# A second pair of PSUM banks for the gate and up matmuls of a quantized FFN, and the pending transposes emitted ahead of the quantizer

## The chip, the cores and the metric

The kernel runs on all 8 cores of one Trainium2 chip. Each core computes one half (2048 tokens) of one of four batch entries, all cores run the same program, and none waits for another. The metric is the device time in microseconds of the slowest core.

## The reference

One layer: a layer norm, multi-head attention with a low-rank key and value, and a gated FFN whose activations and weights are quantized to blocks of 16 FP4 values. The three are added. The change lies in the FFN.

```python
def fp4_quant_dequant(x):                    # blocks of 16 along the last dim
    scale = jnp.maximum(jnp.max(jnp.abs(xb), axis=-1, keepdims=True) / 6.0, 1e-12)
    idx = jnp.searchsorted(_MID, jnp.abs(xb / scale))
    return _GRID[idx] * jnp.sign(xb / scale) * scale
def fp4_linear(x, w):
    return jnp.einsum('bsk,nk->bsn', fp4_quant_dequant(x), fp4_quant_dequant(w))
gate = fp4_linear(xn, w_gate)                # 1024 -> 2816
y = fp4_linear(xn, w_up)                     # 1024 -> 2816
ffn = fp4_linear(jax.nn.silu(gate) * y, w_down)   # 2816 -> 1024
x = x + attention(xn) + ffn
```

## The kernel before

The kernel is written with one instruction queue for each engine, filled by hand in program order (`eb.em`), and with semaphores (`eb.wait`, `then_inc`). An engine runs its queue in order. Earlier stages norm and quantize the tokens, quantize the three weight matrices, do the attention, and leave the residual in HBM. The last stage, from about 2,940 us of the span on, is the FFN.

It runs over two groups `ig` of 1408 hidden columns. For each it loads the quantized weights with transposing DMAs (`wgq_b`, `wuq_b`, `wdq_b`), and then takes the tokens in two halves of 1024. A half has 8 tiles (`tt`) of 128 tokens, and behind them the down projection of the half (L1068, with the add of the residual at L1081).

A tile goes through these steps:

- Three chunks (`ci`) of 512, 512 and 384 hidden columns, here called c0, c1 and c2. For each, TensorE runs 8 gate matmuls into the bank `pg` (L1007) and 8 up matmuls into the bank `py` (L1011). ScalarE takes Silu of `pg` into `gs_c` (L1023), and VectorE multiplies it with `py` into `h_t` (L1027) and counts `hbld` up. `pg` and `py` are the banks `psD0` and `psD1` for each chunk, and chunk number `s_` (counted through the group) waits until `hbld` has the multiply of chunk `s_` - 1 (L1005). `gs_c` has one buffer, so a Silu waits for the multiply before it (L1021).
- `emit_quant` on `h_t`. ScalarE makes Abs and Sign of the whole tile (L189, L192) once c2's multiply is through (L1032). VectorE runs 13 passes over 1408 columns or over the 88 scales: L212, L217 and L222 need only `h_t`, L227 needs Sign, L233 needs Abs, and the rest (L235 to L254) follow one another, up to `hq_t`. Then `hq` counts up.
- `emit_tr`, the transposes of the tile, is put off by one tile: the call stands in `pend_tr` and is emitted one tile later. It emits 11 transposes in groups of 4, 4 and 3 (L962), which take the banks `psA` and `psB` in turn, and for each group an eviction by ScalarE to `hqT_b` (L973). A group waits for the eviction of the group two before it. `emit_tr` emits nothing for VectorE, and `emit_quant` nothing for TensorE.

So TensorE's queue holds, for tile t: c0, c1, c2, and the transposes of tile t-1. ScalarE's holds the three Silus, Abs and Sign of tile t, and the evictions of tile t-1. VectorE's holds the three multiplies and the quantizer. The first tile of a half has no pending transposes, and those of the last are emitted behind it, ahead of the down projection. The banks `psE` and `psF` belong to the attention and stand unused in this stage.

Of the kernel before, what the change touches and what calls it, by code (L numbers as in the profile page):

```python
# [82 lines left out]
def build_program(debug=False, stop_after=9):  # L83
# [46 lines left out]
    S = {}  # L130
# [43 lines left out]
    psD0 = ps_([128, 512], F32, es_ps, "psD0")  # L174
    psD1 = ps_([128, 512], F32, es_ps, "psD1")
    psE = ps_([128, 512], F32, es_ps, "psE")
    psF = ps_([128, 512], F32, es_ps, "psF")
# [131 lines left out]
    eb = EB(nc)  # L309
# [135 lines left out]
    eb = EB(nc)  # L445
# [140 lines left out]
    eb = EB(nc)  # L586
# [251 lines left out]
    eb = EB(nc)  # L838
# [136 lines left out]
    for ig in range(2):  # L975
        i0 = IG[ig]
        if True:
            if ig > 0:
                eb.wait('sync', S['ffdn'], S['ffdn'].n)
            for kc2 in range(KC):  # L980
                S['fw'].n += 16
                eb.em('sync', lambda e, kc2=kc2, i0=i0: e.dma_start(  # L982
                    out=wgq_b[:, kc2, :], in_=WgqN[i0:i0 + 1408, kc2 * 128:(kc2 + 1) * 128], transpose=True).then_inc(S['fw'].h, 16))
            for kc2 in range(KC):
                S['fw'].n += 16
                eb.em('sync', lambda e, kc2=kc2, i0=i0: e.dma_start(  # L986
                    out=wuq_b[:, kc2, :], in_=WuqN[i0:i0 + 1408, kc2 * 128:(kc2 + 1) * 128], transpose=True).then_inc(S['fw'].h, 16))
            for it in range(11):
                S['fw'].n += 16
                eb.em('sync', lambda e, it=it, i0=i0: e.dma_start(  # L990
                    out=wdq_b[:, it, :], in_=WdqN[0:1024, i0 + it * 128:i0 + (it + 1) * 128], transpose=True).then_inc(S['fw'].h, 16))
            eb.wait('tensor', S['fw'], S['fw'].n)
            eb.wait('tensor', S['xqr'], S['xqr'].n)
        hb_base = S['hbld'].n
        for half in range(2):
            toff = half * 1024
            eb.wait('scalar', S['avq'], S['avq'].n)
            for tt in range(8):
                eb.wait('vector', S['aab'], S['aab'].n)
                for ci, (c0, clen) in enumerate(NCH):  # L1000
                    s_ = half * 24 + tt * 3 + ci
                    pg = psD0
                    py = psD1
                    if s_ >= 1:
                        eb.wait('tensor', S['hbld'], hb_base + s_)  # L1005
                    for kc2 in range(KC):
                        eb.em('tensor', lambda e, tt=tt, c0=c0, clen=clen, kc2=kc2, pg=pg, toff=toff: e.matmul(  # L1007
                            pg[:, 0:clen], xqT_sb[:, kc2, toff + tt * 128:toff + (tt + 1) * 128],
                            wgq_b[:, kc2, c0:c0 + clen], start=(kc2 == 0), stop=(kc2 == KC - 1)))
                    for kc2 in range(KC):  # L1010
                        ins = (lambda e, tt=tt, c0=c0, clen=clen, kc2=kc2, py=py, toff=toff: e.matmul(  # L1011
                            py[:, 0:clen], xqT_sb[:, kc2, toff + tt * 128:toff + (tt + 1) * 128],
                            wuq_b[:, kc2, c0:c0 + clen], start=(kc2 == 0), stop=(kc2 == KC - 1)))
                        if kc2 == KC - 1:
                            S['ffh'].n += 1
                            eb.em('tensor', lambda e, ins=ins: ins(e).then_inc(S['ffh'].h, 1))
                        else:
                            eb.em('tensor', ins)
                    eb.wait('scalar', S['ffh'], S['ffh'].n)
                    if S['hbld'].n > 0:  # L1020
                        eb.wait('scalar', S['hbld'], S['hbld'].n)  # L1021
                    S['sil'].n += 1
                    eb.em('scalar', lambda e, clen=clen, pg=pg: e.activation(  # L1023
                        out=gs_c[:, 0:clen], in_=pg[:, 0:clen], func=AF.Silu).then_inc(S['sil'].h, 1))
                    eb.wait('vector', S['sil'], S['sil'].n)
                    S['hbld'].n += 1
                    eb.em('vector', lambda e, c0=c0, clen=clen, py=py: e.tensor_tensor(  # L1027
                        out=h_t[:, c0:c0 + clen], in0=gs_c[:, 0:clen], in1=py[:, 0:clen],
                        op=ALU.mult).then_inc(S['hbld'].h, 1))
                lg = lgq  # L1030
                eb.wait('scalar', S['hq'], S['hq'].n)
                eb.wait('scalar', S['hbld'], S['hbld'].n)  # L1032
                eb.wait('vector', S['hbld'], S['hbld'].n)
                if lg >= 2:
                    eb.wait('vector', S['fftr'], 3 * (lg - 1))
                last = emit_quant(eb, 1408, h_t[:, 0:1408], hq_t[:, lg % 2, 0:1408], PL5, act_abs=True)
                S['hq'].n += 1
                eb.em('vector', lambda e, last=last: last(e).then_inc(S['hq'].h, 1))
                if pend_tr is not None:
                    pend_tr()  # L1040
                pend_tr = (lambda lg=lg, tt=tt, hq_tgt=S['hq'].n: emit_tr(eb, lg, tt, hq_tgt))
                lgq += 1
            if pend_tr is not None:
                pend_tr()
                pend_tr = None
            if debug and half == 0 and ig == 0:
                eb.wait('sync', S['fftrev'], S['fftrev'].n)
                S['out'].n += 16
                eb.em('sync', lambda e: e.dma_start(out=dbg['hq0'], in_=hqT_b[:]).then_inc(S['out'].h, 16))
                eb.wait('vector', S['out'], S['out'].n)  # L1050
            dn_base = S['ffdn'].n
            st_ds = DS['rsd'] if ig == 0 else DS['ost']
            rr_base_i = DS['rr'].cnt
            st_base_i = st_ds.cnt
            for m in range(2):
                DS['rr'].issue(eb, 'sync', rbuf[:, m % 2, :], resid_scr[m * 128:(m + 1) * 128, toff:toff + 1024])
            eb.wait('tensor', S['fftrev'], S['fftrev'].n)
            eb.wait('tensor', S['hbld'], S['hbld'].n)
            DS['rsd'].wait_all(eb, 'vector')
            DS['ost'].wait_all(eb, 'vector')  # L1060
            for m in range(8):
                for n2 in range(2):
                    idx = m * 2 + n2
                    pb = [psC0, psC1][idx % 2]
                    if idx >= 2:
                        eb.wait('tensor', S['ffdn'], dn_base + idx - 1)
                    for it in range(11):
                        ins = (lambda e, m=m, n2=n2, it=it, pb=pb: e.matmul(  # L1068
                            pb[:, :], wdq_b[:, it, m * 128:(m + 1) * 128], hqT_b[:, it, n2 * 512:(n2 + 1) * 512],
                            start=(it == 0), stop=(it == 10)))  # L1070
                        if it == 10:
                            S['avq'].n += 1
                            eb.em('tensor', lambda e, ins=ins: ins(e).then_inc(S['avq'].h, 1))
                        else:
                            eb.em('tensor', ins)
                    eb.wait('vector', S['avq'], S['avq'].n)
                    DS['rr'].wait_for(eb, 'vector', rr_base_i + m)
                    if m >= 2 and n2 == 0:
                        st_ds.wait_for(eb, 'vector', st_base_i + m - 2)
                    S['ffdn'].n += 1  # L1080
                    eb.em('vector', lambda e, m=m, n2=n2, pb=pb: e.tensor_tensor(  # L1081
                        out=obuf[:, m % 2, n2 * 512:(n2 + 1) * 512], in0=rbuf[:, m % 2, n2 * 512:(n2 + 1) * 512],
                        in1=pb[:, :], op=ALU.add).then_inc(S['ffdn'].h, 1))
                eb.wait('sync', S['ffdn'], dn_base + 2 * (m + 1))
                if ig == 0:
                    st_ds.issue(eb, 'sync', resid_scr[m * 128:(m + 1) * 128, toff:toff + 1024], obuf[:, m % 2, :])
                else:
                    st_ds.issue(eb, 'sync', o_out[m * 128:(m + 1) * 128, toff:toff + 1024], obuf[:, m % 2, :])
                if m + 2 < 8:
                    DS['rr'].issue(eb, 'sync', rbuf[:, m % 2, :], resid_scr[(m + 2) * 128:(m + 3) * 128, toff:toff + 1024])  # L1090
            if ig == 0:
                DS['rsd'].wait_all(eb, 'sync')
# [48 lines left out]
```

## Time and profile before

| | us |
|---|---|
| median of the runs | 4250.61 |
| lowest and highest | 4248.65, 4252.58 |
| the profiled execution, slowest core | 4251.97 |
| its span, first to last instruction (core 5) | 4250.3 |
| spans of the 8 cores | 4235.1 to 4250.3 |
| mean granted TensorE clock, each core | 0.829 to 0.830 |

The page gives for each engine its busy time and its share of the span, and then groups of instructions by the line of the kernel, with the engine's idle time ahead of them and the instruction that ended it ("<-" and a name is the releaser). The timeline lists instructions in order of time, alike neighbours merged: start, length, engine, line, operation, output <- inputs, count, and in brackets the idle time of the engine before it. The windows view gives, for stretches of time, the busy time of each engine and the clock granted to TensorE as a share of 2.4 GHz (0.50 is 1.2 GHz).

### The profile page before, as it was taken

How to read it: one execution, taken by the hardware profiler on the slowest of the kernel's cores; microseconds unless marked ns; L12 is line 12 of the kernel's file. 1: busy time of each engine (PE TensorE's matmuls, PEld its weight loads, DVE VectorE, ACT ScalarE, POOL GpSimd, SP SyncE). 2: the span in 40 equal slices, each digit the busy share in tenths (PEclk: the TensorE clock that was granted, in tenths of full speed). 3: DMA queues.
4: the chain of work that ended last, by engine and by line, in shares of the span. 5: the costliest groups of instructions: out<-in, count | busy, mean ns of one | idle time of the engine just before them, and what ended most of it. 6: DMA issues, size and time to landing. Idle time of an engine off the chain costs nothing. (4 is left out here: it accounts for less than half of the span.)

```text
span 4250.3 us, 36150 instructions; the slowest of 8 cores (4235.1 to 4250.3 us)
## 1 busy us (share of the span) xinstructions
PE 2578.5 (61%) x9848; PEld 946.4 (22%) x9848; DVE 2505.1 (59%) x4009; ACT 1185.1 (28%) x1835; POOL 105.7 (2%) x199
## 2 busy tenths in 40 slices
PE   1112185159696978789696969686355555245646
PEld 1112131012121222222121212232122222122222
DVE  7888803757767675857476674231365554365564
ACT  1111121035454545445454545200121111111111
POOL 0000000000000000000000000000000000000000
PEclk9999996569797988979797979778677777677878
DMA  1112130001000010101010000215301002400102
GB/s 50 30 30 66 52 47 1 19 19 36 23 30 28 27 34 19 39 16 38 17 35 19 30 23 21 40 65 168 57 0 50 30 0 82 79 0 25 55 0 69
DMA packets 126529, 156.29 MB, mean 37 GB/s; under 512 B 77824, under 2 KB 88320, under 8 KB 124288
## 3 DMA queue, kind: packets, MB, share of 16 engines
q1 hardware_dynamic: 110368, 127.56, 10.8%
q0 software_dynamic: 15968, 26.42, 2.6%
q8 instruction: 89, 1.46, 0.2%
q14 instruction: 104, 0.85, 0.1%
HBM read 98.89 MB, written 46.66 MB: 34 GB/s over the span
## 5 line engine op out<-in xcount | busy, mean ns | idle before, releaser
L1007 PE MATMUL psD<-wgq_b,xqT_sb 128*128 128x512 bf16 (+1 forms) x768 | 252.4, 491 | 503.5 <-DVE h_t L1027 376.7
L765 ACT ACTIVATE pbuf<-psA,negB_col 128x512 bf16<-128x512 f32 x512 | 351.4, 686 | 349.4 <-PE psA L751 349.4
L765 ACT ACTIVATE pbuf<-psB,negB_col 128x512 bf16<-128x512 f32 x512 | 351.2, 686 | 289.0 <-PE psB L751 288.1
L1027 DVE TENSOR_TENSOR h_t<-gs_c,psD 128x512 f32<-128x512 f32 (+1 forms) x96 | 61.5, 641 | 460.7 <-ACT gs_c L1023 460.7
L212 DVE TENSOR_REDUCE pbm<-wbuf 128x32 f32<-128x512 f32 (+1 forms) x136 | 91.1, 670 | 401.3 <-DMA WdqN<-wqout 163.0
L1023 ACT ACTIVATE gs_c<-psD 128x512 f32<-128x512 f32 (+1 forms) x96 | 53.9, 562 | 972.5 <-PE psD L1011 972.5
L781 PE MATMUL psC<-pbuf,V_h 128*128 128x512 bf16 x1024 | 311.1, 386 | 17.9 <-ACT pbuf L765 17.8
L781 PE MATMUL psD<-pbuf,V_h 128*128 128x512 bf16 x1024 | 304.5, 379 | 27.5 <-ACT pbuf L765 27.5
L751 PE MATMUL psA<-qT_all,kT_h 128*128 128x512 bf16 x1024 | 316.7, 392 | 0.4 <-DVEq L723 0.4
L751 PE MATMUL psB<-qT_all,kT_h 128*128 128x512 bf16 x1024 | 314.3, 389 | 0.0
L1007 PEld LDWEIGHTS psD<-wgq_b,xqT_sb 128*128 128x128 bf16 x768 | 89.1, 122 | 645.9 <-issue 623.5
L781 PE MATMUL psE<-pbuf,V_h 128*1 128x512 bf16 x512 | 196.0, 383 | 0.0
L781 PE MATMUL psF<-pbuf,V_h 128*1 128x512 bf16 x512 | 193.0, 377 | 0.0
L1011 PE MATMUL psD<-wuq_b,xqT_sb 128*128 128x512 bf16 (+1 forms) x768 | 187.1, 391 | 0.0
L1068 PE MATMUL psC<-hqT_b,wdq_b 128*128 128x512 bf16 x704 | 159.9, 391 | 5.3 <-ACT hqT_b L973 3.3
L342 PE MATMUL psA<-ident_t,xq_f 128*128 128x128 f32 x64 | 17.4, 428 | 232.4 <-DVE xq_f L254 232.4
L781 PEld LDWEIGHTS psC<-pbuf,V_h 128*128 128x128 bf16 x1024 | 98.6, 99 | 150.2 <-issue 40.2
L781 PEld LDWEIGHTS psD<-pbuf,V_h 128*128 128x128 bf16 x1024 | 97.7, 98 | 153.4 <-issue 40.8
L1081 DVE TENSOR_TENSOR obuf<-rbuf,psC 128x512 f32<-128x512 f32 x64 | 43.8, 688 | 136.9 <-PE psC L1068 123.9
L342 PE MATMUL psA<-ident_t,xn_scr 128*128 128x128 f32 x128 | 34.8, 428 | 136.9 <-DVE xn_scr L385 136.9
L888 PE MATMUL psC<-o_all,wo_b 128*128 128x512 bf16 x512 | 112.8, 384 | 1.5 <-DVE o_all L870 1.5
L1011 PEld LDWEIGHTS psD<-wuq_b,xqT_sb 128*128 128x128 bf16 x768 | 83.0, 108 | 103.8 <-issue 48.3
(204 smaller groups left out, 4242.9 us busy)
## 6 DMA issues: line engine op xcount, KB each, us to landing
xbuf<-x_tok SPq DMA_DIRECT2D x16, 1024.0 KB, 5.4
rbuf<-resid_scr SPq DMA_DIRECT2D x32, 512.0 KB, 5.6
wbuf<-Wg SPq DMA_DIRECT2D x44, 256.0 KB, 2.8
wbuf<-Wu SPq DMA_DIRECT2D x44, 256.0 KB, 2.7
wbuf<-Wd SPq DMA_DIRECT2D x40, 256.0 KB, 2.7
xt_buf<-xT_own SPq DMA_DIRECT2D x8, 1024.0 KB, 7.9
resid_scr<-rstage SPq DMA_DIRECT2D x8, 1024.0 KB, 5.2
resid_scr<-obuf SPq DMA_DIRECT2D x16, 512.0 KB, 2.8
```

What stands on the lines that cost most here:

```text
L212: t_bm = op(lambda e: e.tensor_reduce(out=pbm[:, 0:NB], in_=src3, axis=AX.X, op=ALU.max, apply_absolute_value=True))
L342: ins = (lambda e, c=c, j=j, pbank=pbank, src_tile=src_tile: e.transpose(pbank[:, j * 128:(j + 1) * 128], src_tile[:, c * 128:(c + 1) * 12 ...
L751: ins = (lambda e, h=h, qq=qq, kc=kc, m=m, pb=pb: e.matmul(pb[:, :], kT_h[:, m, kc * 128:(kc + 1) * 128], qT_all[:, 2 * h + m, qq * 512:(q ...
L765: eb.em('scalar', lambda e, cglob=cglob, pb=pb: e.activation(out=pbuf[:, cglob % 2, :], in_=pb[:, :], func=AF.Exp, bias=negB_col[:], scale ...
L781: ins = (lambda e, kc=kc, cg=cg, lo=lo, hi=hi, dstp=dstp, dsl=dsl: e.matmul(dstp[dsl, 0:512], V_h[:, kc, lo:hi], pbuf[:, cg % 2, :], start ...
L888: ins = (lambda e, m=m, n=n, kc=kc, pb=pb: e.matmul(pb[:, :], wo_b[:, kc, m * 128:(m + 1) * 128], o_all[:, kc, n * 512:(n + 1) * 512], sta ...
L1007: eb.em('tensor', lambda e, tt=tt, c0=c0, clen=clen, kc2=kc2, pg=pg, toff=toff: e.matmul(pg[:, 0:clen], xqT_sb[:, kc2, toff + tt * 128:tof ...
L1011: ins = (lambda e, tt=tt, c0=c0, clen=clen, kc2=kc2, py=py, toff=toff: e.matmul(py[:, 0:clen], xqT_sb[:, kc2, toff + tt * 128:toff + (tt + ...
L1023: eb.em('scalar', lambda e, clen=clen, pg=pg: e.activation(out=gs_c[:, 0:clen], in_=pg[:, 0:clen], func=AF.Silu).then_inc(S['sil'].h, 1))
L1027: eb.em('vector', lambda e, c0=c0, clen=clen, py=py: e.tensor_tensor(out=h_t[:, c0:c0 + clen], in0=gs_c[:, 0:clen], in1=py[:, 0:clen], op= ...
L1068: ins = (lambda e, m=m, n2=n2, it=it, pb=pb: e.matmul(pb[:, :], wdq_b[:, it, m * 128:(m + 1) * 128], hqT_b[:, it, n2 * 512:(n2 + 1) * 512] ...
L1081: eb.em('vector', lambda e, m=m, n2=n2, pb=pb: e.tensor_tensor(out=obuf[:, m % 2, n2 * 512:(n2 + 1) * 512], in0=rbuf[:, m % 2, n2 * 512:(n ...
```

## The change

There are two edits in the tile loop of the FFN. The pair of banks alternates between (`psD0`, `psD1`) and (`psE`, `psF`), and a chunk waits for the multiply of the chunk two before it. And the pending transposes of the tile before are emitted ahead of `emit_quant` and not behind it.

```diff
@@ -999,10 +999,9 @@
                 for ci, (c0, clen) in enumerate(NCH):
                     s_ = half * 24 + tt * 3 + ci
-                    pg = psD0
-                    py = psD1
-                    if s_ >= 1:
-                        eb.wait('tensor', S['hbld'], hb_base + s_)
+                    pg, py = [(psD0, psD1), (psE, psF)][s_ % 2]
+                    if s_ >= 2:
+                        eb.wait('tensor', S['hbld'], hb_base + s_ - 1)
                     for kc2 in range(KC):
@@ -1033,11 +1032,11 @@
                 if lg >= 2:
                     eb.wait('vector', S['fftr'], 3 * (lg - 1))
+                if pend_tr is not None:
+                    pend_tr()
                 last = emit_quant(eb, 1408, h_t[:, 0:1408], hq_t[:, lg % 2, 0:1408], PL5, act_abs=True)
                 S['hq'].n += 1
                 eb.em('vector', lambda e, last=last: last(e).then_inc(S['hq'].h, 1))
-                if pend_tr is not None:
-                    pend_tr()
                 pend_tr = (lambda lg=lg, tt=tt, hq_tgt=S['hq'].n: emit_tr(eb, lg, tt, hq_tgt))
```

## Rows read from the trace of the kernel before

**Rows 1.** The page, TensorE's busy time in the whole span:

```profile
PE 2578.5 (61%) x9848; PEld 946.4 (22%) x9848; DVE 2505.1 (59%) x4009; ACT 1185.1 (28%) x1835; POOL 105.7 (2%) x199
```

**Rows 2.** Groups by line, 2900 to 4250 us; busy, mean | idle before, releasers:

```profile
L1007 PE MATMUL psD<-wgq_b,xqT_sb 128*128 128x512 bf16 (+1 forms) x768 | 252.4, 491 | 503.5 <-DVE h_t L1027 376.7 <-DMA wdq_b<-WdqN 126.7
...
L1027 DVE TENSOR_TENSOR h_t<-gs_c,psD 128x512 f32<-128x512 f32 (+1 forms) x96 | 61.5, 641 | 460.7 <-ACT gs_c L1023 460.7
```

**Rows 3.** The view of line 1027, who waited for it (us, times):

```profile
  PE psD L1007: 376.7, 68
```

**Rows 4.** Timeline, one following tile, first the tile before's L227:

```profile
3509.43 1.59 DVE L227 TENSOR_TENSOR PL5pK<-PL5pK,pscale 128x1408 f32<-128x1408 f32 x1
...
3525.55 0.68 DVE L1027 TENSOR_TENSOR h_t<-gs_c,psD 128x512 f32<-128x512 f32 x1
...
3526.37 3.42 PE L1007 MATMUL psD<-wgq_b,xqT_sb 128*128 128x512 bf16 x8 [9.56 <-DVE h_t L1027]
...
3531.67 0.60 ACT L1023 ACTIVATE gs_c<-psD 128x512 f32<-128x512 f32 x1 [14.12 <-PE psD L1011]
3532.37 0.69 DVE L1027 TENSOR_TENSOR h_t<-gs_c,psD 128x512 f32<-128x512 f32 x1 [6.15 <-ACT gs_c L1023]
...
3533.21 1.46 PE L1007 MATMUL psD<-wgq_b,xqT_sb 128*128 128x384 bf16 x8 [1.68 <-DVE h_t L1027]
...
3534.50 1.46 PE L1011 MATMUL psD<-wuq_b,xqT_sb 128*128 128x384 bf16 x8
...
3536.24 0.60 PE L962 MATMUL psB<-ident_t,hq_t 128*128 128x128 f32 x4
3536.71 0.55 DVE L1027 TENSOR_TENSOR h_t<-gs_c,psD 128x384 f32<-128x384 f32 x1 [3.65 <-ACT gs_c L1023]
...
3538.64 1.36 ACT L192 ACTIVATE PL5pK<-h_t 128x1408 f32<-128x1408 f32 x1
...
3539.91 0.56 ACT L973 CAST hqT_b<-psA 128x512 bf16<-128x512 f32 x1
3540.13 1.59 DVE L227 TENSOR_TENSOR PL5pK<-PL5pK,pscale 128x1408 f32<-128x1408 f32 x1
...
3540.62 0.87 PE L962 MATMUL psA<-ident_t,hq_t 128*128 128x128 f32 x3 [3.78 <-ACT hqT_b L973]
...
3541.86 0.48 ACT L973 CAST hqT_b<-psA 128x384 bf16<-128x384 f32 x1 [0.90 <-PE psA L962]
```

**Rows 5.** Timeline, the opening tiles of three halves:

```profile
3013.10 0.69 DVE L1027 TENSOR_TENSOR h_t<-gs_c,psD 128x512 f32<-128x512 f32 x1 [77.43 <-ACT gs_c L1023]
...
3013.93 1.89 PE L1007 MATMUL psD<-wgq_b,xqT_sb 128*128 128x512 bf16 x8 [1.63 <-DVE h_t L1027]
...
3015.66 1.89 PE L1011 MATMUL psD<-wuq_b,xqT_sb 128*128 128x512 bf16 x8
...
3302.90 1.89 PE L1007 MATMUL psD<-wgq_b,xqT_sb 128*128 128x512 bf16 x8
...
3307.36 0.69 DVE L1027 TENSOR_TENSOR h_t<-gs_c,psD 128x512 f32<-128x512 f32 x1 [3.44 <-ACT gs_c L1023]
...
3308.20 1.89 PE L1007 MATMUL psD<-wgq_b,xqT_sb 128*128 128x512 bf16 x8 [1.69 <-DVE h_t L1027]
...
3312.66 0.69 DVE L1027 TENSOR_TENSOR h_t<-gs_c,psD 128x512 f32<-128x512 f32 x1 [4.61 <-ACT gs_c L1023]
3313.47 1.10 PEld L1007 LDWEIGHTS psD<-wgq_b,xqT_sb 128*128 128x128 bf16 x8 [2.15 <-issue]
...
3654.80 3.57 PE L1007 MATMUL psD<-wgq_b,xqT_sb 128*128 128x512 bf16 x8 [54.77 <-DMA wdq_b<-WdqN]
...
3658.17 2.41 PE L1011 MATMUL psD<-wuq_b,xqT_sb 128*128 128x512 bf16 x8
...
3661.43 0.69 DVE L1027 TENSOR_TENSOR h_t<-gs_c,psD 128x512 f32<-128x512 f32 x1 [60.54 <-ACT gs_c L1023]
```

**Rows 6.** Windows; after each engine's busy time the granted clock, DMA share, GB/s:

```profile
3243.50:3257.00 13.50, 0.87 (x3) 0.50 (x3) 13.22 (x10) 0.96 (x2) 0.00 (x0) 0.50 0.00 1
3370.60:3376.00 5.40, 5.33 (x13) 1.95 (x14) 0.00 (x0) 0.00 (x0) 0.00 (x0) 0.51 0.00 0
3378.50:3381.30 2.80, 2.76 (x18) 1.79 (x19) 0.00 (x0) 0.00 (x0) 0.00 (x0) 1.00 0.00 0
```

**Rows 7.** Timeline, evictions in another following tile:

```profile
3353.49 0.56 ACT L973 CAST hqT_b<-psA 128x512 bf16<-128x512 f32 x1
...
3354.81 0.48 ACT L973 CAST hqT_b<-psA 128x384 bf16<-128x384 f32 x1 [0.27 <-PE psA L962]
```

## The prediction

> **What bounds the kernel now.** I read the page first: over the whole span TensorE is busy 61% and VectorE 59% [rows 1], so neither engine is the bound by its share; what counts is who waits for whom in the stage that the diff touches. Grouping the last 1,350 us by line [rows 2], the reader is to see that the first matmuls of a chunk (L1007) stand behind 376.7 us of idle TensorE that ended with the multiply of L1027, and that the multiply stands behind 460.7 us of idle VectorE that ended with the Silu of L1023, which needs the matmuls. The view of line 1027 says that TensorE waited for it 68 times [rows 3]. The two engines take turns. The timeline of one tile [rows 4] shows it in order. I call Q the start of the multiply of chunk c0 and E the end of the multiply of chunk c2.
>
> From Q = 3525.55 the matmuls of c1 start at 3526.37, are followed by its Silu, and c1's multiply starts at 3532.37: 6.82 us after Q, in which VectorE has nothing to do. Then c2 starts at 3533.21 and its multiply ends at E = 3536.71 + 0.55 = 3537.26: 4.89 us after c1's multiply began. The quantizer follows. Its pass at L227 starts at 3540.13, which is E + 2.87, after Abs and Sign on ScalarE (Sign ends at 3538.64 + 1.36 = 3540.00). From that pass to the next Q the earlier tile shows 3509.43 to 3525.55, 16.12 us of VectorE without a hole. One period is 6.82 + 4.89 + 2.87 + 16.12 = 30.70 us. There are 32 tiles: 4 that open a half, and 28 that follow another tile.
>
> The 6.82 are not one number. In the opening tile of a half the same turn takes 3307.36 to 3312.66, 5.30 us [rows 5], with matmuls at the high level of the clock; in the 28 others TensorE has been idle for about 10 us (9.56 in rows 4) and restarts low: granted 0.51, which is the 1.2 GHz level, for the stretch in which such a c1 runs, and 1.00 (2.4 GHz) for the c2 behind it [rows 6]. The surplus from this follows from the 460.7 us: take off the opening waits (77.43 + 60.54 + 2 x 3.44 = 144.9), 32 waits for c2 of 3.65 (116.8) and 4 for an opening c1 of 4.61 (18.4), and 180.6 us are left for 28 tiles, 6.45 each; with the multiply's 0.69 that is 7.14, so 1.84 us above 5.30 [rows 2, 4, 5].
>
> **Part 1, the second pair of banks.** A chunk now waits for the multiply two chunks back. In a following tile c0 and c1 of tile t+1 both may run during the quantizer of tile t: c1's condition is tile t's last multiply, E itself. They need 32 matmuls of 512 columns. At the high level eight take 3302.90 to 3304.62 = 1.72, so 6.9 us; at the low level eight take 3654.80 to 3658.17 = 3.37, so 13.5 us [rows 5]. They start when the last transposes are through, some 1.3 us after E, and are done by E + 8.2 to E + 14.8; Q comes at E + 2.87 + 16.12 = E + 19, or later. So c1 is hidden at either clock, by 4 us or more. What is left after Q is the gate of c2 only: c2 still needs c0's multiply. c0's multiply at Q lets c2 start at Q + 0.82, the distance that c1 has now, and while c2's matmuls run, c1's Silu and multiply (0.69) pass beside them. The 5.30 us turn goes: **28 x 5.30 = 148.4 us**. If the cover were gone it would all come back.
>
> The surplus doesn't go with it. Now c2 is the first work after TensorE's idle time. The idle time is from E + 8.2 or E + 14.8 to Q + 0.82, at least 5 us and at most 13; the third transpose group, after 3.78 us of idle time [rows 4], ran in a stretch granted 0.50 [rows 6]. I therefore have c2 start low. Its surplus is between 0 (clock stays high) and the whole chunk low: 16 matmuls of 384 columns take 2 x (3534.50 - 3533.21) = 2.58 us high [rows 4], and by the ratio 3.37/1.72 some 5.0 low, a surplus of 2.5 at most. I take the surplus of the present c1, 1.84: it is a low stretch of some 3.6 us, and that fits inside 5.0. So the surplus moves from c1 to c2 at no change.
>
> **The opening tiles** (4): c0 starts at 3302.90, and c2 0.84 us (3532.37 to 3533.21, [rows 4]) after c1's multiply of 3312.66, at 3313.50 [rows 5]. With two pairs c1 follows c0 at once and c2 follows c1 (c0's multiply, 3307.36 + 0.69, is over before c1's matmuls are), so c2 starts at 3302.90 + 6.9 = 3309.8, 3.7 us sooner. **4 x 3.7 = 14.8 us.** They have no pending transposes, so part 2 costs them nothing.
>
> **Part 2, the pending transposes before the quantizer.** emit_quant emits nothing for TensorE and emit_tr nothing for VectorE, nor any DMA; SP's and POOL's queues don't change. The only order that changes is ScalarE's: the three evictions (L973) of tile t-1 now stand ahead of Abs and Sign of tile t. Nothing waits for the evictions at once; what is queued behind them is Abs and Sign, and L227 and L233 wait for those. ScalarE's wait for c2's multiply (L1032) still stands ahead of both, so the evictions can't use the time before E. They cost their full length. Their first takes the place of Abs, at E + 0.10. The first two transpose groups are over by then (3536.24 + 0.60 against E = 3537.26) and the third waits for the first eviction. Now the third eviction starts 3541.86 - 3539.91 = 1.95 us after the first with the third group at the low level; in another tile, 1.32 us after it [rows 7]. The next ScalarE instruction starts about 0.4 us behind the third. So Abs and Sign come 1.32 + 0.39 = 1.71 us later, or 1.95 + 0.39 = 2.34. L227 starts 0.13 us after Sign ends, so there is no slack: the whole delay reaches the quantizer's end. I take 1.71, because the transposes will follow a c2 that has been running for some 4 us and the wait for the eviction is about 1 us, not 3.78. **28 x 1.71 = 47.9 us lost.** What it gives, an earlier third transpose group, shortens nothing, since c0 and c1 are hidden anyway.
>
> Nothing else is on the path: the pass lengths of the quantizer, the down projection, and the weight loads stay. Sum: -148.4 - 14.8 + 47.9 = **-115.3 us** against the span of 4250.3: 4135.0. The profiled execution took 4251.97 and the median shown is 4250.61, 0.3 from the span, so I forecast **4135 us**. A following tile's period goes from about 31.0 to 27.4 us.
>
> **The rivals.**
> (B) TensorE's clock stays high over the idle time, so c2 has no surplus: 28 x 1.84 = 51.5 us more, 4083 us. For it: TensorE works 7 to 13 us in one block. Against: 3.78 us of idle time were enough for a low third group. 0.10.
> (C) Everything is low: c2 with a surplus of 2.5 and the transposes at the low level. Per tile -5.30 + 2.34 + 0.66 = -2.30; 28 x 2.30 + 14.8 = 79, so 4171 us. For it: a c2 of 5 us low would end before the clock rises, since a c1 stretch of 5.40 us was granted 0.51 [rows 6]. Against: most c1 have a smaller surplus. 0.12. The Trainium skill ("TensorE: Matmul & The Clock Gate", A second HAM failure mode: psum-queue depth-cycling) says that cycling through PSUM banks in every iteration makes the clock swing between its levels; by that rule alone it would be this case, 4171.
> (D) The second pair brings nothing and only the evictions' delay is paid: 28 x 1.71 = 48, so 4298 us. It is so if c0 and c1 don't both fit in the quantizer: they would have to take over 19 us, against 13.5 at worst. 0.04. The Trainium skill (same page, HAM oscillation — how this bites in real kernels) tells of a kernel in which PSUM double-buffering "gave no further gain". That speaks against this change; the trace bears it out only for a kernel that doesn't wait for its banks, and this one waits 68 times [rows 3].
> (E) Slower: Sign comes so late that it eats the gain. The place is ScalarE's queue between E and Abs: each eviction waits for TensorE. If the third transposes were served only after the next c0 and c1, Sign would be 13.5 us later still: 28 x (13.5 + 1.71 - 5.30) - 14.8 = +263, 4513 us. It ends 2% slower once the delay passes (85 + 14.8)/28 + 5.30 = 8.9 us. Against it: in TensorE's queue the transposes stand ahead of c0. 0.03.
>
> **How the numbers follow.** My forecast has 0.71, with delay and surplus spread about the chosen values: 1 us a tile is 28 us, so its own range is about 4105 to 4165. The range 4100 to 4175 takes in C; it leaves out B, D and E, 0.17. About 2% (85 us, 4166 to 4336) is what a measurement of this kernel can tell from no change. Faster: 0.71 + 0.10 = 0.81. Same: C and D, 0.16. Slower: 0.03.
>
> **What would show it.** In the changed trace: the idle time before L1027 falls from 460.7 by over 150 us; between two Q lie about 27.4 us; c1's multiply starts within 2 us of c0's; c2's matmuls start 0.8 us after Q in a stretch granted near 0.5, and E follows in some 6.7 us; L227 starts at E + 4.6 and not E + 2.87; the three L973 stand ahead of L189. The prediction is wrong if the L973 casts spread over more than 2.5 us, if c2 runs at 1.00 throughout, or if the passes at L238 to L254 grow beyond 1.62 us with more matmuls beside them.

## The result and the profile after

The changed kernel's profiled execution took 4137.42 us, its span was 4135.9 us (core 6). Against the kernel before, the ratio is 0.977, with a 95% interval from 0.972 to 0.982: faster by 2.3%, with an interval that reaches across the 2% mark, so it isn't settled that the gain is 2% or more. The median over all its runs is 4183.07 us and the interval is wide because in several of them TensorE of one die was granted a lower clock than that of the other; what follows therefore goes by spans of profiles (for one kernel below, core 0 in the place of the slowest core), and the two profiled executions stand at 4137.42 / 4251.97 = 0.973.

The page, engines' busy time and the granted clock in 40 slices:

```profile
PE 2498.6 (60%) x9675; PEld 936.7 (23%) x9848; DVE 2508.3 (61%) x4009; ACT 1187.2 (29%) x1835; POOL 106.1 (3%) x199
...
PEclk9999997559799797979799897968777877777877
```

VectorE is busy nearly as long as before [rows 1]. The page lists 9675 matmul records where the one before has 9848, with 9848 weight loads in both: the matmuls of the two kernels are the same in number, some records are missing here, and TensorE's busy time isn't compared. What changed is the idle time. Groups by line for the last stage (busy, mean | idle before, releaser); L1026 is the line that was L1027:

```profile
L227 DVE TENSOR_TENSOR PL5pK<-PL5pK,pscale 128x1408 f32<-128x1408 f32 x32 | 51.9, 1623 | 47.0 <-ACT PL5pK L192 47.0
...
L1026 DVE TENSOR_TENSOR h_t<-gs_c,psD 128x512 f32<-128x512 f32 (+1 forms) x48 | 30.8, 642 | 209.8 <-ACT gs_c L1022 209.8
L1026 DVE TENSOR_TENSOR h_t<-gs_c,psF 128x512 f32<-128x512 f32 (+1 forms) x48 | 30.8, 641 | 86.2 <-ACT gs_c L1022 86.2
```

The idle time of VectorE ahead of the multiply was 460.7 us [rows 2] and is now 209.8 + 86.2 = 296.0. Against this stand 47.0 us ahead of L227, where the kernel before had 0.2. Together 460.9 became 343.0, 117.9 us less; the span is 114.4 us shorter. These sums also hold the waits of VectorE ahead of the first multiply of a half, 144.9 us before and 141.3 now, nearly all of it behind weight loads, and these waits differ from core to core. In the 28 following tiles alone, the timelines of the two cores give 178.6 us ahead of c1's multiply and 104.2 ahead of c2's before, and 22.2 and 114.1 now. One following tile of the changed kernel, with Q at 3443.15:

```profile
3443.15 0.68 DVE L1026 TENSOR_TENSOR h_t<-gs_c,psD 128x512 f32<-128x512 f32 x1
...
3443.97 2.72 PE L1006 MATMUL psD<-wgq_b,xqT_sb 128*128 128x384 bf16 x8 [13.29 <-DVE h_t L1026]
...
3444.62 0.69 DVE L1026 TENSOR_TENSOR h_t<-gs_c,psF 128x512 f32<-128x512 f32 x1 [0.79 <-ACT gs_c L1022]
...
3448.60 0.60 PE L962 MATMUL psA<-ident_t,hq_t 128*128 128x128 f32 x4
3449.07 0.55 DVE L1026 TENSOR_TENSOR h_t<-gs_c,psD 128x384 f32<-128x384 f32 x1 [3.76 <-ACT gs_c L1022]
3449.77 0.59 ACT L973 CAST hqT_b<-psB 128x512 bf16<-128x512 f32 x1 [0.80 <-DVE h_t L1026]
...
3450.50 0.52 PE L962 MATMUL psB<-ident_t,hq_t 128*128 128x128 f32 x3 [1.30 <-ACT hqT_b L973]
...
3451.11 0.48 ACT L973 CAST hqT_b<-psB 128x384 bf16<-128x384 f32 x1 [0.27 <-PE psB L962]
3451.48 1.38 ACT L189 ACTIVATE PL5pA<-h_t 128x1408 f32<-128x1408 f32 x1
...
3454.23 1.63 DVE L227 TENSOR_TENSOR PL5pK<-PL5pK,pscale 128x1408 f32<-128x1408 f32 x1 [1.65 <-ACT PL5pK L192]
...
3470.38 0.68 DVE L1026 TENSOR_TENSOR h_t<-gs_c,psF 128x512 f32<-128x512 f32 x1
```

The multiply of c1 now starts 1.47 us after Q, where it took 6.82 [rows 4]: c1's matmuls were done. c2 starts at Q + 0.82, after 13.29 us of idle TensorE, and E is 3449.07 + 0.55 = 3449.62, 6.47 us after Q. Then come the three evictions, from E + 0.15 on, the third 1.34 us behind the first, and Abs stands behind them. L227 starts at E + 4.61, where it stood at E + 2.87. The next Q is 16.15 us later. The period is 27.23 us. The clock (the number behind the engines' busy times) in three stretches, c2, then the matmuls of the next c0 and c1, then the idle time ahead of the next c2:

```profile
3443.90:3448.00 4.10, 4.03 (x16) 2.04 (x16) 0.69 (x1) 0.60 (x1) 0.00 (x0) 0.59 0.00 0
3450.00:3458.00 8.00, 7.37 (x34) 3.41 (x35) 6.03 (x6) 4.46 (x6) 0.00 (x0) 1.00 0.01 2
3465.00:3471.00 6.00, 0.00 (x0) 0.00 (x0) 5.65 (x5) 0.00 (x0) 0.00 (x0) 0.50 0.00 0
```

c0 and c1 of the next tile run wholly at the 2.4 GHz level, the level falls to 1.2 GHz while TensorE is idle, and c2 meets it there. The surplus on c2 isn't the same in all tiles. These are the multiplies of c2 in four of the seven following tiles of the first half; the bracket is the wait for c2:

```profile
3044.97 0.55 DVE L1026 TENSOR_TENSOR h_t<-gs_c,psF 128x384 f32<-128x384 f32 x1 [5.04 <-ACT gs_c L1022]
...
3072.90 0.56 DVE L1026 TENSOR_TENSOR h_t<-gs_c,psD 128x384 f32<-128x384 f32 x1 [4.45 <-ACT gs_c L1022]
...
3182.72 0.56 DVE L1026 TENSOR_TENSOR h_t<-gs_c,psD 128x384 f32<-128x384 f32 x1 [3.87 <-ACT gs_c L1022]
...
3210.05 0.55 DVE L1026 TENSOR_TENSOR h_t<-gs_c,psF 128x384 f32<-128x384 f32 x1 [3.85 <-ACT gs_c L1022]
```

The wait falls from 5.04 through 4.45 to 3.87 and 3.85. It is 2.17 with c2 at the high level (shown below).

### The profile page after: what moved, and what is told of

The parts are those of the page before. It is cut to its first block and busy times, and to the rows that moved or that the text cites. A ratio compares the mean times of both kernels' runs of the same rounds, so it can differ in the third digit from the quotient of the medians.

```text
span 4135.9 us, 35975 instructions; the slowest of 8 cores (4119.1 to 4135.9 us)
## 1 busy us (share of the span) xinstructions
PE 2498.6 (60%) x9675; PEld 936.7 (23%) x9848; DVE 2508.3 (61%) x4009; ACT 1187.2 (29%) x1835; POOL 106.1 (3%) x199
## 3 DMA queue, kind: packets, MB, share of 16 engines
q8 instruction: 89, 1.46, 0.1%
## 5 line engine op out<-in xcount | busy, mean ns | idle before, releaser
L781 PE MATMUL psC<-pbuf,V_h 128*128 128x512 bf16 x976 | 300.7, 386 | 17.9 <-ACT pbuf L765 17.8
L781 PE MATMUL psD<-pbuf,V_h 128*128 128x512 bf16 x976 | 294.1, 379 | 27.5 <-ACT pbuf L765 27.5
L1006 PE MATMUL psD<-wgq_b,xqT_sb 128*128 128x512 bf16 (+1 forms) x375 | 100.4, 421 | 282.2 <-DVE h_t L1026 159.4
L1006 PE MATMUL psE<-wgq_b,xqT_sb 128*128 128x512 bf16 (+1 forms) x371 | 101.7, 428 | 217.7 <-DVE h_t L1026 217.0
L781 PE MATMUL psE<-pbuf,V_h 128*1 128x512 bf16 x512 | 196.0, 383 | 7.0
L1022 ACT ACTIVATE gs_c<-psD 128x512 f32<-128x512 f32 (+1 forms) x48 | 27.0, 562 | 578.4 <-PE psD L1010 320.3
L1026 DVE TENSOR_TENSOR h_t<-gs_c,psD 128x512 f32<-128x512 f32 (+1 forms) x48 | 30.8, 642 | 209.8 <-ACT gs_c L1022 209.8
L342 PE MATMUL psA<-ident_t,xq_f 128*128 128x128 f32 x64 | 17.4, 428 | 232.4 <-DVE xq_f L254 232.4
L1006 PEld LDWEIGHTS psD<-wgq_b,xqT_sb 128*128 128x128 bf16 x384 | 41.2, 110 | 331.9 <-issue 303.7
L1022 ACT ACTIVATE gs_c<-psE 128x512 f32<-128x512 f32 (+1 forms) x48 | 26.9, 561 | 277.0 <-DVE h_t L1026 191.3
```

Of the source, the lines that this page charges most:

```text
L342: ins = (lambda e, c=c, j=j, pbank=pbank, src_tile=src_tile: e.transpose(pbank[:, j * 128:(j + 1) * 128], src_tile[:, c * 128:(c + 1) * 12 ...
L781: ins = (lambda e, kc=kc, cg=cg, lo=lo, hi=hi, dstp=dstp, dsl=dsl: e.matmul(dstp[dsl, 0:512], V_h[:, kc, lo:hi], pbuf[:, cg % 2, :], start ...
L1022: eb.em('scalar', lambda e, clen=clen, pg=pg: e.activation(out=gs_c[:, 0:clen], in_=pg[:, 0:clen], func=AF.Silu).then_inc(S['sil'].h, 1))
```

## The experiments

Some of the kernels do unneeded work on top of the reference's, as said. The table has the sum of VectorE's idle time ahead of the multiplies of all tiles, the part of it that stands ahead of c2's multiply in the 28 following tiles (added up from the timeline), and the idle time ahead of L227, for the last stage of the core named by its span. The first sum holds 141 to 148 us of waits ahead of the first multiply of the four halves, so what c2 costs is read from the second. The spans of the eight cores of one execution differ by 12 to 22 us in all of these kernels but one, so a few us between two spans say nothing.

| kernel | before the multiplies, us | c2, following tiles, us | before L227, us | span, us |
|---|---|---|---|---|
| before | 460.7 | 104.2 | 0.2 | 4250.3 |
| changed | 296.0 | 114.1 | 47.0 | 4135.9 |
| second pair alone | 308.7 | 123.0 | 0.2 | 4094.2 |
| order alone | 479.0 | 104.2 | 47.0 | 4321.1 |
| changed, 52 matmuls in the gap | 272.9 | 86.4 | 47.0 | 4117.4 |
| changed, 60 matmuls in the gap | 248.1 | 61.1 | 47.0 | 4085.2 |
| changed, Abs of 512 more | 301.7 | 114.9 | 62.9 | 4155.2 |
| changed, Abs of 1408 more | 307.1 | 119.0 | 86.8 | 4188.1 |
| changed, evictions ahead of E | 319.1 | 130.5 | 23.6 | 4137.3 |
| third pair, old order | 202.8 | 19.7 | 0.2 | 4000.3 |
| third pair, Silus apart, old order | 159.2 | 0.0 | 0.2 | 3941.8 (core 0) |
| the same, new order | 163.7 | 0.0 | 56.9 | 4010.1 |

### The two edits apart

The second pair of banks alone; the order is that of the kernel before:

```diff
...
+                    pg, py = [(psD0, psD1), (psE, psF)][s_ % 2]
+                    if s_ >= 2:
+                        eb.wait('tensor', S['hbld'], hb_base + s_ - 1)
```

> Only the second pair of banks; the pending transposes stay behind the quantizer, as before the change. Theory 1 (the terms add): the changed kernel's L227 sat idle 47.0 us for Sign (28 x 1.68), and without the moved evictions this goes: span 4135.9 - 47 = 4089 us, L227 at E + 2.87. Theory 2 (the low-clock surplus of c2 depends on when c2 starts and takes part of the gain back; it lay between 1.6 and 2.9 us a tile in the changed kernel and can be 2.5): up to 28 x 0.9 = 25 us come back, span 4089 to 4115. Rival (the order of evictions and Sign doesn't matter): 4136 us.

The median was 4097.58 us, the ratio to before 0.964 (0.960 to 0.968), the span 4094.2. Groups by line of this kernel:

```profile
L227 DVE TENSOR_TENSOR PL5pK<-PL5pK,pscale 128x1408 f32<-128x1408 f32 x32 | 51.1, 1598 | 0.2 <-issue 0.2
...
L1026 DVE TENSOR_TENSOR h_t<-gs_c,psD 128x512 f32<-128x512 f32 (+1 forms) x48 | 30.8, 642 | 219.1 <-ACT gs_c L1022 219.1
L1026 DVE TENSOR_TENSOR h_t<-gs_c,psF 128x512 f32<-128x512 f32 (+1 forms) x48 | 30.8, 641 | 89.6 <-ACT gs_c L1022 89.6
```

The 47.0 us ahead of L227 are gone, so they belong to the order. The span is 41.7 us shorter than with both edits, and not 47, since the waits for c2 grew by 8.9 us, from 114.1 to 123.0. (The other 3.6 us are within what the cores differ by.) In its timeline the waits for c2 of four tiles in a row don't settle; they swing:

```profile
3300.46 0.55 DVE L1026 TENSOR_TENSOR h_t<-gs_c,psF 128x384 f32<-128x384 f32 x1 [4.51 <-ACT gs_c L1022]
...
3326.86 0.56 DVE L1026 TENSOR_TENSOR h_t<-gs_c,psD 128x384 f32<-128x384 f32 x1 [4.69 <-ACT gs_c L1022]
...
3352.39 0.56 DVE L1026 TENSOR_TENSOR h_t<-gs_c,psF 128x384 f32<-128x384 f32 x1 [3.81 <-ACT gs_c L1022]
...
3378.78 0.55 DVE L1026 TENSOR_TENSOR h_t<-gs_c,psD 128x384 f32<-128x384 f32 x1 [4.68 <-ACT gs_c L1022]
```

The rival that the order doesn't matter (4136 us) is out. The new order alone, with one pair of banks:

```diff
+                if pend_tr is not None:
+                    pend_tr()
                 last = emit_quant(eb, 1408, h_t[:, 0:1408], hq_t[:, lg % 2, 0:1408], PL5, act_abs=True)
...
```

> Only the order: one pair of banks as before, the pending transposes and their evictions ahead of the quantizer. Theory 1 (the terms add): 28 x 1.71 to 2.34 us more than before, span 4298 to 4316 us, slower than before by 1.1 to 1.5%. Theory 2 (a later start of c1 shortens its low-clock stretch): the surplus of c1 (1.4 to 2.6 us in the kernel before) falls by part of the delay, span 4265 to 4298 us. Rival (an earlier third transpose group lets c0 start sooner and helps): 4250 us or less.

The profiled span was 4321.1 us, 70.8 us more than before (1.7%; a single execution), and 5 us beyond theory 1's range. Its groups by line:

```profile
L1027 DVE TENSOR_TENSOR h_t<-gs_c,psD 128x512 f32<-128x512 f32 (+1 forms) x96 | 61.5, 641 | 479.0 <-ACT gs_c L1023 479.0
...
L227 DVE TENSOR_TENSOR PL5pK<-PL5pK,pscale 128x1408 f32<-128x1408 f32 x32 | 51.9, 1623 | 47.0 <-ACT PL5pK L192 47.0
```

The delay of L227 costs the same 47.0 us as in the changed kernel. Theory 2 had the wrong sign here: the surplus of c1 didn't fall but grew: its waits in the following tiles rose from 178.6 to 196.0, by 17.4 us. That c0 can start sooner brought nothing.

### The low clock on c2

The changed kernel with matmuls in TensorE's idle time ahead of c2, 52 in the first version:

```diff
+                    if tt >= 1 and ci == 1:
+                        for fz in range(52):
+                            eb.em('tensor', lambda e, tt=tt, toff=toff: e.matmul(
+                                psC0[:, :], xqT_sb[:, 0, toff + tt * 128:toff + (tt + 1) * 128],
+                                wgq_b[:, 0, 0:512], start=True, stop=True))
```

> The changed kernel with 52 more matmuls of 512 columns behind c1's matmuls in each following tile, into a bank that nothing reads; the result is unchanged by them. They take up about 11.2 us of the 13.3 us in which TensorE sits idle ahead of c2. If that idle time is what makes c2 start at the low clock, c2 is granted near 1.00, the surplus of 1.7 us a tile goes, a period falls from 27.3 to 25.6 us, and the span is 4135.9 - 28 x 1.8 = 4085 us. If the clock isn't kept high by them (they would then take 22 us), c2 starts late by some 8 us and the span is above 4300 us. If the surplus has another cause, 4136 us.

The ratio was 0.969 (0.965 to 0.973), the span 4117.4: 18.5 us less than the changed kernel, a third of what was expected; the waits for c2 fell by 27.7 us, from 114.1 to 86.4. In 11 of the 28 tiles the wait for c2 was 2.17 us, and c2 ran high. In the others c2 was low in part or from its start on. This is one of them, after an idle time of 2.06 us, and the granted clock in its first and second part:

```profile
3455.34 1.48 PE L1006 MATMUL psE<-wgq_b,xqT_sb 128*128 128x384 bf16 x8 [2.06 <-DVE h_t L1031]
```

```profile
3455.30:3457.00 1.70, 1.66 (x10) 1.00 (x11) 0.69 (x1) 0.58 (x1) 0.00 (x0) 0.90 0.00 0
3457.00:3459.20 2.20, 2.20 (x9) 1.07 (x8) 0.00 (x0) 0.00 (x0) 0.00 (x0) 0.50 0.00 0
```

c2 began at the high level and was moved to the low one in the middle. The same 2.06 us of idle time stood ahead of most of the c2 that ran high throughout, and the ones at 3615.05 and 3877.72 ran high behind 2.99 and 2.98 us. So the length of the idle time alone doesn't say which tile gets the low clock. The next run leaves almost none (range(60) in the place of range(52)).

> The changed kernel with 60 more matmuls behind c1's in each following tile, where the run with 52 left 2.06 us of idle TensorE ahead of c2 and half of its tiles still had c2's up matmuls at the low clock (Q to E 6.2 to 6.6 us, against 4.88 in the others). 60 leave about 0.3 us. If idle time ahead of c2 is the whole cause of the surplus, all 28 tiles have Q to E = 4.9 us, the periods are 25.6 us and the span is 4135.9 - 28 x 1.9 = 4083 us. If c2's clock falls for another reason, half of the tiles keep their surplus and the span stays at 4110 to 4120 us.

The ratio was 0.961 (0.958 to 0.964), the span 4085.2 us, against 4083 expected. One tile, the added matmuls, c2 and its multiply, and then the groups by line:

```profile
3406.51 13.11 PE L1020 MATMUL psC<-wgq_b,xqT_sb 128*128 128x512 bf16 x60
...
3419.96 1.46 PE L1006 MATMUL psD<-wgq_b,xqT_sb 128*128 128x384 bf16 x8 [0.34 <-DVE h_t L1031]
...
3423.46 0.55 DVE L1031 TENSOR_TENSOR h_t<-gs_c,psD 128x384 f32<-128x384 f32 x1 [2.17 <-ACT gs_c L1027]
```

```profile
L1031 DVE TENSOR_TENSOR h_t<-gs_c,psD 128x512 f32<-128x512 f32 (+1 forms) x48 | 30.8, 641 | 192.4 <-ACT gs_c L1027 192.4
L1031 DVE TENSOR_TENSOR h_t<-gs_c,psF 128x512 f32<-128x512 f32 (+1 forms) x48 | 30.7, 641 | 55.7 <-ACT gs_c L1027 55.7
```

With 0.34 us of idle time left, c2's eight gate matmuls last 1.46 us where they lasted 2.72, and the wait for c2 is 2.17 us. So it is in 27 of the 28 following tiles; in the first of the stage it is 2.52. The granted clock around the c2 that starts at 3368.32:

```profile
3367.80:3370.80 3.00, 2.67 (x17) 1.54 (x17) 1.06 (x2) 0.60 (x1) 0.00 (x0) 1.00 0.00 0
```

The waits for c2 fell by 114.1 - 61.1 = 53.0 us, 1.89 for each of the 28 tiles. That is the surplus, and its cause is the idle time ahead of c2: 60 matmuls of no use in a tile make the span 50.7 us shorter.

### What a delay ahead of Sign costs

The changed kernel with one more Abs of 512 columns, and then of 1408, into a tile `dly` that nothing reads:

```diff
...
                 if pend_tr is not None:
                     pend_tr()
+                eb.em('scalar', lambda e: e.activation(out=dly[:, 0:512], in_=h_t[:, 0:512], func=AF.Abs))
```

> The changed kernel with one more ScalarE pass (Abs of 512 columns into a tile that nothing reads) between the evictions and Abs of every tile, about 0.5 us. Theory 1 (the terms add): 32 x 0.5 = +16 us, 4152 us, periods of 27.8 us. Theory 2 (c2's low-clock stretch ends at a time that doesn't move with c2's start, so a later start shortens it): the surplus falls by the delay, the periods stay at 27.3 us and the span at 4136 to 4140 us.

> As the run with the pass of 512 columns more, but with 1408 columns, about 1.3 us a tile. Theory 1 (the terms add): 32 x 1.3 = +42 us, 4178 us. Theory 2 (a later start shortens the low stretch): c2's settled surplus of 1.7 us would fall to 0.4, periods of 27.3 us and 4136 to 4145 us; if a low stretch can't be that short, the period jumps beyond 27.3 + 1.3 = 28.6 us, and the span is above 4178 us.

The ratios were 0.978 (0.974 to 0.982) and 0.985 (0.983 to 0.988), the spans 4155.2 and 4188.1, 19.3 and 52.2 us above the changed kernel. Theory 1 had 4152 and 4178. The groups of L227, first with 512 columns:

```profile
L227 DVE TENSOR_TENSOR PL5pK<-PL5pK,pscale 128x1408 f32<-128x1408 f32 x32 | 52.0, 1626 | 62.9 <-ACT PL5pK L192 62.9
```

and with 1408:

```profile
L227 DVE TENSOR_TENSOR PL5pK<-PL5pK,pscale 128x1408 f32<-128x1408 f32 x32 | 52.0, 1626 | 86.8 <-ACT PL5pK L192 86.8
```

The wait for Sign grew by 15.9 and 39.8 us, as theory 1 has it. The waits for c2 didn't shrink: they grew by 0.8 us, which is nothing clear, and by 4.9. Theory 2, that a later c2 makes up for the delay, fell. Single tiles do it (the wait falls from tile to tile, as in the rows of the changed kernel), but then one jumps back to the full surplus, and the mean surplus stays at 1.9 and 2.1 us ((114.9 - 61.1) / 28 and (119.0 - 61.1) / 28, with the 61.1 us of the filled gap).

The other direction, the transposes emitted ahead of ScalarE's wait for c2's multiply:

```diff
+                if pend_tr is not None:
+                    pend_tr()
                 eb.wait('scalar', S['hq'], S['hq'].n)
                 eb.wait('scalar', S['hbld'], S['hbld'].n)
                 eb.wait('vector', S['hbld'], S['hbld'].n)
                 if lg >= 2:
                     eb.wait('vector', S['fftr'], 3 * (lg - 1))
-                if pend_tr is not None:
-                    pend_tr()
```

> The changed kernel with the pending transposes emitted one step earlier still, ahead of ScalarE's wait for c2's multiply (L1032). If that wait is what makes the evictions cost their full length, the first two now start behind c2's Silu, 0.7 us before E, and the third 0.8 us sooner: L227 at E + 3.8 and not E + 4.6, span 4135.9 - 28 x 0.8 = 4113 us. If only the count of evictions ahead of Abs matters, or the surplus takes the gain, 4130 to 4136 us.

The span was 4137.3 us, 1.4 us from the changed kernel's. Groups by line:

```profile
L227 DVE TENSOR_TENSOR PL5pK<-PL5pK,pscale 128x1408 f32<-128x1408 f32 x32 | 51.9, 1623 | 23.6 <-ACT PL5pK L192 23.6
...
L1026 DVE TENSOR_TENSOR h_t<-gs_c,psD 128x512 f32<-128x512 f32 (+1 forms) x48 | 30.8, 642 | 223.9 <-ACT gs_c L1022 223.9
L1026 DVE TENSOR_TENSOR h_t<-gs_c,psF 128x512 f32<-128x512 f32 (+1 forms) x48 | 30.8, 641 | 95.2 <-ACT gs_c L1022 95.2
```

The wait for Sign halved, from 47.0 to 23.6, by 0.84 us a tile, as expected from the order. And the waits for c2 rose from 114.1 to 130.5, so of the 23.4 us won 16.4 were lost again there. The other 7 us don't show in the span either: over the eight cores its mean is 4128.0 us, where the changed kernel has 4127.3. Most of the tiles settled at nearly the full surplus (5.38 us between the multiplies of c1 and c2, where c2 at the high level has 2.86). In both kernels the period comes to rest at about 27.3 us, so a shorter wait for Sign is made up by a longer wait for c2. That is measured; by what rule a start that moves by 0.8 us moves the surplus by as much stays open. The surplus was larger with a later start (order alone, Abs of 1408 more) and with an earlier one (second pair alone, this one).

### Taking c2 off the path

A third pair of banks, `psC0` and `psC1`, which in this stage only the down projection behind the tiles uses, with the transposes behind the quantizer as before the change:

```diff
+                    pg, py = [(psD0, psD1), (psE, psF), (psC0, psC1)][s_ % 3]
+                    if s_ >= 3:
+                        eb.wait('tensor', S['hbld'], hb_base + s_ - 2)
+                    if tt == 0 and ci == 2:
+                        eb.wait('tensor', S['ffdn'], S['ffdn'].n)
```

> The transposes behind the quantizer as before the change, and a third pair of banks (psC0, psC1, which the down projection uses after the tiles) so that c2's matmuls also run during the quantizer of the tile before. Left between Q and E are multiply c0, Silu c1, multiply c1, Silu c2, multiply c2: 1.48 + 1.48 + 0.55 = 3.5 us, and no low clock on the path. Period 16.15 + 2.87 + 3.5 = 22.5 us, 8.5 less than before: 4250.3 - 28 x 8.5 - 4 x 3.7 = 3997 us. Rival (the low clock comes back, since 48 matmuls at the low level take 18.5 us and with the transposes nearly fill the period): up to 4060 us.

Median 4000.08 us, ratio 0.941 (0.939 to 0.942), span 4000.3, where 3997 was expected. The period of the following tiles was 22.4 us. The low clock is still there, but on the next tile's c0, behind the transposes: its eight gate matmuls began in a stretch granted 0.67 (3352.00 to 3357.00), and c1 and c2 behind it ran at 1.00, with nobody waiting for them. And with a place in `gs_c` for each chunk:

```diff
-    gs_c = sb("gs_c", [128, 512], F32, es_b5)
+    gs_c = sb("gs_c", [128, 1408], F32, es_b5)
...
-                        eb.wait('scalar', S['hbld'], S['hbld'].n)
+                        eb.wait('scalar', S['hbld'], S['hbld'].n - 2)
...
-                        out=gs_c[:, 0:clen], in_=pg[:, 0:clen], func=AF.Silu).then_inc(S['sil'].h, 1))
+                        out=gs_c[:, c0:c0 + clen], in_=pg[:, 0:clen], func=AF.Silu).then_inc(S['sil'].h, 1))
```

> As the kernel with three pairs, and gs_c with a place for each chunk, so that all three Silus run during the quantizer too. Between Q and E only three multiplies are left, about 2.1 us: period 16.15 + 2.87 + 2.1 = 21.1 us, span 4250.3 - 28 x 9.9 - 14.8 = 3958 us. VectorE is then busy all through a tile but for the wait for Sign. Rival (TensorE or ScalarE becomes late): Silu c0 to c2 of the next tile aren't done at Q, and the period stays at 22.5 us.

Median 3948.99 us, ratio 0.928 (0.927 to 0.930), where a span of 3958 was expected. This is the fastest of the kernels. Its groups by line, core 0:

```profile
L1028 DVE TENSOR_TENSOR h_t<-gs_c,psF 128x512 f32<-128x512 f32 x32 | 21.8, 682 | 11.1 <-ACT gs_c L1024 11.1
L1028 DVE TENSOR_TENSOR h_t<-gs_c,psD 128x512 f32<-128x512 f32 x32 | 21.8, 681 | 140.9 <-ACT gs_c L1024 140.9
...
L1028 DVE TENSOR_TENSOR h_t<-gs_c,psC 128x384 f32<-128x384 f32 x32 | 17.6, 549 | 7.2 <-ACT gs_c L1024 7.2
```

The three multiplies follow one another, 0.6 us apart, and what is left belongs to the four opening tiles: the 140.9 us ahead of c0's are 74.29 + 59.76 + 2 x 3.44. The period is 20.7 us, nearly all of it VectorE's own passes.

The same kernel with the new order:

> The kernel with three pairs and a place for each Silu, with the pending transposes ahead of the quantizer, as in the changed kernel. There is no low-clock stretch on the path that could take the delay up, so the order's cost shows bare: 28 x 1.7 = 47 us more than its neighbour with the transposes behind. Rival (the evictions can run at E at no cost to Sign, or something else sets the period): the same time as its neighbour.

Ratio 0.944 (0.942 to 0.947), span 4010.1. Its core 0 took 4003.9 us, 62.1 more than core 0 of its neighbour, where 47 were expected. Its timeline around the evictions, with Q at 3364.58 and E at 3366.33:

```profile
3364.92 1.09 PE L962 MATMUL psA<-ident_t,hq_t 128*128 128x128 f32 x4 [9.84 <-DVE hq_t L254]
...
3366.47 0.59 ACT L973 CAST hqT_b<-psA 128x512 bf16<-128x512 f32 x1 [10.74 <-DVE h_t L1028]
...
3367.20 0.87 PE L962 MATMUL psA<-ident_t,hq_t 128*128 128x128 f32 x3 [0.34 <-ACT hqT_b L973]
...
3368.16 0.48 ACT L973 CAST hqT_b<-psA 128x384 bf16<-128x384 f32 x1 [0.62 <-PE psA L962]
...
3371.29 1.62 DVE L227 TENSOR_TENSOR PL5pK<-PL5pK,pscale 128x1408 f32<-128x1408 f32 x1 [2.01 <-ACT PL5pK L192]
```

The delay is larger than in the changed kernel: L227 at E + 4.96, its wait 2.01 us. The transposes come first after TensorE's 9.84 us of idle time here, so they run low (granted 0.50 from 3364.90 to 3368.20): 0.87 us for the third group, where the changed kernel has 0.52, and the third eviction starts 1.69 us after the first, and not 1.34. The prediction's upper price for such low transposes was 2.34; here the delay is 4.96 - 2.87 = 2.09. With no c2 on the path to blur it, the order costs what the wait says, 57 of the 62.1 us; 3.1 of the rest stand ahead of the opening multiplies (144.0 against 140.9 on core 0).

## Why the prediction came out right

**What bounds.** The prediction read two engines that wait for each other, and its first step, 28 turns of 5.30 us removed, is borne out by c1's multiply at Q + 1.47: c2 at the high level leaves waits of 0.79 and 2.17 us, where c1 and c2 at the high level had 4.61 and 3.65 before, 5.30 less. The opening tiles are as worked out. c0, c1 and c2 of one, and its last multiply:

```profile
3275.12 1.89 PE L1006 MATMUL psD<-wgq_b,xqT_sb 128*128 128x512 bf16 x8
...
3278.57 1.89 PE L1006 MATMUL psE<-wgq_b,xqT_sb 128*128 128x512 bf16 x8
...
3282.03 1.46 PE L1006 MATMUL psD<-wgq_b,xqT_sb 128*128 128x384 bf16 x8
...
3285.54 0.55 DVE L1026 TENSOR_TENSOR h_t<-gs_c,psD 128x384 f32<-128x384 f32 x1 [1.80 <-ACT gs_c L1022]
```

c2 starts 6.91 us after c0, where 6.9 was foretold. (The prediction takes 1.72 us for eight matmuls at the high level from a row that isn't among its rows; it is this one of the kernel before, which follows the matmuls at 3302.90. [Rows 5] give 1.73 by 3013.93 and 3015.66. The start of c2 that it works out as 3313.50 is in [rows 5] only by its weight loads, at 3313.47.)

```profile
3304.62 1.89 PE L1011 MATMUL psD<-wuq_b,xqT_sb 128*128 128x512 bf16 x8
```

The terms were -148.4 and -14.8 us. In the following tiles the waits for c1 and c2 fell from 178.6 + 104.2 to 22.2 + 114.1, by 146.5; in the opening tiles, without the waits for weights, by 14.7.

**The surplus moved and didn't go.** Taken as 1.84 us a tile from the kernel before; the filled gap shows 1.89 in the changed one. (Before it was (178.6 - 28 x 4.61) / 28 = 1.77: the prediction gave all 32 waits for c2 the 3.65 us of one row, and two of them are longer.) Rival B, the clock staying high, priced at 4083, is what the kernel with 60 matmuls in the gap does: 4085.2. It needs TensorE to be fed; c0 and c1 in one block don't suffice, as the row of 3465.00 with its 0.50 shows.

**The evictions.** Taken as 1.71 us, 47.9 in all; measured 47.0 of wait for Sign, and the second pair alone shows it gone. The choice of the shorter value was right, and for the reason given: the third group came after 1.30 us of idle TensorE and ran in 0.52 us. Where c2 no longer ran ahead of the transposes, the delay went up to 2.09.

**The sum.** -115.3 against -114.4 in the span, 4135 against 4135.9. The mechanism was right, but that the sum came within 1 us is luck: eight cores of this one execution span 17 us, and the parts interact through the surplus. Between the changed kernel and the second pair alone it shifts by 8.9 us, in the run with the evictions ahead of E by 16.4, and there a gain of 23.4 us left nothing in the span. The prediction had each term stand by itself, and carried the surplus over unchanged from c1 to c2 with no reason from the rows but that it would fit; it could have come out up to 2.5 us a tile, some 18 us more in all. The range, 35 us down and 40 us up, covers that.

**The rivals.** C (everything low, 4171) didn't come: the level rises within c2 (granted 0.59 over it), and the transposes behind it ran high. The rule of the Trainium skill ("TensorE: Matmul & The Clock Gate", A second HAM failure mode: psum-queue depth-cycling) names the swing of the clock, and the trace agrees that it swings (0.50 to 1.00 in each period), but so it did with one pair, and the matmuls of c0 and c1 ran at 1.00. D (no gain) fell: the second pair alone brought 156 us. The same page's sentence (HAM oscillation — how this bites in real kernels) that double-buffering in PSUM "gave no further gain" doesn't carry over to this kernel, in which TensorE waited 376.7 us for its banks. E (Sign so late that the gain is eaten) has the right place and the wrong size: 1.7 us a tile, where 8.9 are needed.

## What to carry to other kernels

When two engines take turns, look at what is ready when the slow one comes back: each buffer that lets one more piece be ready takes its whole turn off the period (5.3 us a tile for the second pair, and for the third the turn of c2 with its low clock), until only the slow engine's own passes are left. Work that nobody waits for belongs behind the work that someone waits for, on every queue: three evictions of half a microsecond, one step too early, cost 42 us of the 156. And where a clock surplus stands on the path, don't add up small terms beside it as if they stood alone: 0.84 us a tile won ahead of it brought nothing. Count a clock surplus with the first matmuls after the idle time, whichever they are; it moves on with the wait.

## What was not expected of the hardware

- After only 2.06 us of idle TensorE, in a stream that was otherwise dense, c2 kept the high level in 11 of 28 tiles; in the others it was at the low level in part or from its start on. With 0.34 us the wait for c2 was that of the high level in 27 of 28.
- The low stretch of c2 isn't the same in tiles that are otherwise alike. In the changed kernel the waits for c2 shrink from tile to tile towards 3.85 us, in the second pair alone they swing (3.81 and 4.69), and a start of the quantizer's passes 0.84 us sooner left the span where it was.
- 60 added matmuls a tile that compute nothing of use made the span 50.7 us shorter.
